# Layer norm of an attention and feed-forward kernel: the mean is subtracted from a ring of four moment buffers instead of being negated first

## What is computed

```python
x = L0_attn_x                                   # (2, 2048, 256), float32
m, v = x.mean(-1), x.var(-1)
xn = (x - m) / sqrt(v + 1e-5)                   # the layer norm, used by both branches
s = attention(xn, Wq, Wk, Wv, Wo)               # 16 heads of 16, q and k scaled to unit length,
                                                # causal window of 128 keys, linear bias
g = silu(ffn(xn, w_gate, w_up, w_down))         # 704 hidden columns; inputs and weights rounded
                                                # to a 4-bit grid in blocks of 16
out = x + s * g
```

## Time and profile before

| | |
|---|---|
| time, 3 runs | 507.41 us (507.39 to 507.47) |
| span of the profiled execution, first to last instruction | 507.1 us |
| busy: PE, DVE, ACT, POOL | 471.6 (93%), 429.2 (85%), 402.6 (79%), 415.7 (82%) us |
| PE's granted clock, mean over the span | 0.983 of full |
| shares of the chain that ended last | PE 82%, issue, DVE, ACT and POOL 1% each |
| `neg_mean` instructions | 32 of 929 on POOL |

### The profile page before, as it was taken

The page is one execution under the profiler, slowest core; times in us unless marked ns, Lnnn a source line. Parts: engine busy times, 40 slices in busy tenths (PEclk is TensorE's granted clock), DMA queues, the critical chain, the costliest instruction groups (busy, mean ns, idle before and its releaser), DMA issues.

```text
span 507.1 us, 14045 instructions
## 1 busy us (share of the span) xinstructions
PE 471.6 (93%) x4990; PEld 409.0 (81%) x4990; DVE 429.2 (85%) x865; ACT 402.6 (79%) x584; POOL 415.7 (82%) x929
## 2 busy tenths in 40 slices
PE   0367989999999999999999999999999999999997
PEld 0356768888888888888989888888898888888886
DVE  4989988889888888888989888888898888887685
ACT  1456988988888888888887888888888888888952
POOL 6554679899989989899997898989999899888651
PEclk9967999999999999999999999999999999999999
DMA  8211011222322113222222222222222221122100
GB/s 303 81 43 43 13 29 45 64 74 75 74 59 48 51 36 65 64 63 64 65 64 45 62 34 53 63 55 53 53 54 54 52 46 29 37 53 53 44 22 32
DMA packets 78276, 29.35 MB, mean 58 GB/s; under 512 B 67712, under 2 KB 77696, under 8 KB 78208
## 3 DMA queue, kind: packets, MB, share of 16 engines
q1 hardware_dynamic: 77920, 28.39, 22.2%
q10 hardware_dynamic: 288, 0.08, 0.1%
HBM read 7.49 MB, written 4.19 MB: 23 GB/s over the span
## 4 chain that ended last, share of the span: by engine, by line
PE 82%; DVE 1%; ACT 1%; issue 1%; POOL 1%; DVEq 0%; POOLq 0%
PE gt L348 12%; PE up L348 11%; PE bank_b L592 11%; PE gt L545 11%; PE bank_q L348 8%; PE bank_b L354 6%; PE gt L354 6%; PE scores L499 5%; PE gt L567 5%; PE bank_b L348 4%; PE gt L549 1%; PE up L499 1%; PE scores L348 0%; PE up L567 0%; ACT pv_t L1196 0%
## 5 line engine op out<-in xcount | busy, mean ns | idle before, releaser
L1318 ACT ACTIVATE probs<-scores 128x1024 f32<-128x1024 f32 (+1 forms) x101 | 102.5, 1015 | 3.4 <-PE scores L499 2.1
L1503 POOL TENSOR_SCALAR_AFFINE_SELECT probs<-probs 128x512 f32<-128x512 f32 x128 | 81.4, 638 | 3.0 <-ACT probs L1318 2.7
L1510 POOL TENSOR_SCALAR_AFFINE_SELECT probs<-probs 128x512 f32<-128x512 f32 x120 | 75.9, 634 | 3.7
L592 PE MATMUL bank_b<-probs,vals 128*32 128x128 f32 x1952 | 59.7, 274 | 0.4 <-DVE vals L928 0.3
L592 PEld LDWEIGHTS bank_b<-probs,vals 128*32 128x32 f32 x1952 | 51.4, 110 | 7.0 <-DVE vals L928 6.1
L1196 ACT ACTIVATE qk_stack<-bank_q 128x512 f16<-128x512 f32 x64 | 35.2, 597 | 21.8 <-DVE bank_q L907 21.8
L781 DVE TENSOR_TENSOR xT_lo<-gt,xT_hi 128x512 fp32r<-128x512 f32 (+1 forms) x34 | 22.3, 657 | 31.1 <-ACT xT_hi L1196 31.1
L545 PE MATMUL gt<-wdn_hi,hT_hi 128*128 128x256 f32 x160 | 47.8, 299 | 0.6 <-DVE hT_lo L833 0.6
L545 PE MATMUL gt<-wdn_hi,hT_lo 128*128 128x256 f32 x160 | 45.1, 282 | 0.0
L545 PE MATMUL gt<-wdn_lo,hT_hi 128*128 128x256 f32 x160 | 45.0, 281 | 0.0
L348 PE MATMUL up<-wgu_hi,xT_hi 128*128 128x352 f32 x124 | 43.2, 349 | 0.3 <-DVE h_grid L822 0.3
(11 more groups left out here) (219 smaller groups left out, 1650.9 us busy)
## 6 DMA issues: line engine op xcount, KB each, us to landing
out<-y SPq DMA_DIRECT2D x32, 128.0 KB, 2.0
x_all<-x SPq DMA_DIRECT2D x20, 128.0 KB, 2.0
x_all<-x SPq DMA_DIRECT2D x3, 512.0 KB, 4.0
x_all<-wproj SPq DMA_DIRECT2D x1, 768.0 KB, 6.7
dn_raw<-wd SPq DMA_DIRECT2D x1, 704.0 KB, 8.3
probs<-wg SPq DMA_DIRECT2D x1, 640.0 KB, 5.3
probs<-wu SPq DMA_DIRECT2D x1, 640.0 KB, 7.2
qk_slots<-qk_stack SPq DMA_TRANSPOSE x32, 3.7
```

Source lines behind the costliest of these rows:

```text
L592: done = e.matmul(pv_bank(i)[32 * n:32 * n + 32, grp * P:(grp + 1) * P], va, pr, start=part == 0, stop=part == 1 or final(i))
L1318: e.activation(probs[j % P_BUFS][:, grp, :, side(j), :], score_banks(j, grp)[:, :, :, side(j), :].rearrange("p b e h q -> p (b e) h q"), A ...
L1503: e.affine_select(out=own, in_=own, compare_op=ALU.is_ge, fill=0.0, base=0, pattern=[[0, GRP], [-1, P]], channel_multiplier=1).then_inc(s_ ...
L1510: e.affine_select(out=part, in_=part, compare_op=ALU.is_gt, fill=0.0, base=0, pattern=[[0, GRP], [1, P]], channel_multiplier=-1).then_inc( ...
```

## The change

`moments` becomes a ring of four buffers, indexed as `xn` is. `x_norm` takes the mean from there and subtracts it, so that the second instruction of `ln_parts`, the buffer `neg_mean` and the semaphore `s_neg_mean` go. `ln_moments(t)` waits only for the `x_norm` that was the last reader of its buffer, four tiles back, and for no call of POOL in the first four tiles. `x_norm(t)` waits for `s_moments` where it waited for `s_neg_mean`.

```diff
-        moments = sb("moments", [P, 2])
-        neg_mean = sb("neg_mean", [P, 2])
+        moments = sb("moments", [P, XN_BUFS, 2])
...
         def mean_col(t):
-            return neg_mean[:, 0:1] if t == 0 else neg_mean[:, 1:2]
+            return moments[:, t % XN_BUFS, 0:1]
...
             def ln_moments(t):
                 e.wait_ge(s_stats, t + 1)
-                if t >= 1:
-                    e.wait_ge(s_var, t)
-                    e.wait_ge(s_neg_mean, t)
-                e.bn_aggr(moments[:], stats[:]).then_inc(s_moments, 1)
+                if t >= XN_BUFS:
+                    e.wait_ge(s_xn, t - XN_BUFS + 1)
+                e.bn_aggr(moments[:, t % XN_BUFS, :], stats[:]).then_inc(s_moments, 1)
...
                 if t >= 2:
                     e.wait_ge(s_rs, roots(t - 3, Z_ARG))
                     e.wait_ge(s_xn, t)
-                e.tensor_scalar(ss[:, ln_col(t)], moments[:, 1:2], LN_EPS, None, ALU.add).then_inc(s_var, 1)
-                e.tensor_scalar(mean_col(t), moments[:, 0:1], -1.0, None, ALU.mult).then_inc(s_neg_mean, 1)
+                e.tensor_scalar(ss[:, ln_col(t)], moments[:, t % XN_BUFS, 1:2], LN_EPS, None, ALU.add).then_inc(s_var, 1)
...
             def x_norm(t):
                 e.wait_ge(s_rs, roots(max(t - 2, -1), ROOT))
-                e.wait_ge(s_neg_mean, t + 1)
+                e.wait_ge(s_moments, t + 1)
                 if t >= XN_BUFS:
                     e.wait_ge(s_tr_x, t - XN_BUFS + 1)
                     e.wait_ge(s_xc, chain(t - XN_BUFS, NORM))
                 e.tensor_scalar(xn[t % XN_BUFS][:], x_all[:, t % X_RING, :], mean_col(t), rsq[0][:, ln_col(t)],
-                                ALU.add, ALU.mult).then_inc(s_xn, 1)
+                                ALU.subtract, ALU.mult).then_inc(s_xn, 1)
```

More of the change, by code:

```diff
@@ L220, in build @@
             [sem(f"{n}{i}") for i in range(4)] for n in ("scores", "exp", "mask_own", "mask_prev"))
-        s_stats, s_moments, s_var, s_neg_mean, s_xn, s_rs, s_ss, s_floor, s_unit = (
-            sem(n) for n in ("s_stats", "s_moments", "s_var", "s_neg_mean", "s_xn", "s_rs", "s_ss", "s_floor", "s_unit"))
+        s_stats, s_moments, s_var, s_xn, s_rs, s_ss, s_floor, s_unit = (
+            sem(n) for n in ("s_stats", "s_moments", "s_var", "s_xn", "s_rs", "s_ss", "s_floor", "s_unit"))
         s_qk_sq, s_hi_q, s_hi_k, s_lo_qk, s_vals = (
```

## The result

The changed kernel takes 519.21 us (median of 5 runs, 518.74 to 520.12) against 507.47 us; the ratio is 1.0222, 95% interval 1.0205 to 1.0238. I had forecast 506.7. The profiled execution has a span of 518.4 us. A ratio and the quotient of two medians weigh single executions differently, and the two can be 0.1% apart.

What follows compares the result with a forecast made beforehand. PE was taken to bound the loop, with a relay of engines at the start and a POOL run ending at 72.80 us. Gains of 0.4 + 0.3 = 0.7 us gave 507.4 - 0.7 = 506.7 us, range 505.3 to 507.8.

Steps and rivals of the forecast that it cites:

- The subtraction reads the same sizes: `x_norm` on POOL: stays at 0.55 us; if 0.1 more, only tiles 0 and 4 stand on the path, costing 0.2.
- The loop: 25 `neg_mean` of 0.30 us removed from POOL between 75 and 434 us: worth 0, bounds nothing and 7.5 us.
- rival A: POOL paces the loop, so its removed work counts there: 8.2 us gained, 499.2 us; 7 in 100.
- POOL's results are just in time: Loop: POOL's root ends 0.08 us before `unit` in turn 12, yet PE does not wait for POOL.
- The start: Path to `xn(0)`: a wait of 0.22 us and a step of 0.29 go; 0.52 gained, 0.4 left by 62 us.
- `neg_mean(5)`: POOL instruction at 67.99 us, ahead of `root(3)` and `unit(3)`: its removal reaches PE whole, 0.3 us, lower bound 0.23.
- B: Start-up: return to full clock comes after `gate_mm(0)`, costing 1.6 us more, less the 0.7: 508.3 us; 10 in 100.
- C: Start-up: half-clock stretch ends before the `up` and first q/k products of 43.90 to 50.50: 504.7 us; 10 in 100.
- the low end of my sum: Lower bound of the whole gain: 0.5 us, from 0.3 at the start and 0.23 for `neg_mean(5)`.
- The new waits: `ln_moments(t)` waits for `x_norm(t - 4)`, `x_norm(t)` for `s_moments`: nothing queues behind either.

Runs made afterwards that it cites:

- experiment 1: The changed kernel with the layer norm's last step adding the mean instead of subtracting it, so it computes something else: 504.91 us, ratio 0.9954 to the kernel before.
- experiment 3: The kernel before with the negation done a second time on GpSimd, into an unread column, for tiles 7 to 31: 508.89 us, ratio 1.0018.
- experiment 2: The kernel before with the mean copied by a factor of +1 and subtracted in the layer norm's last step; buffers, waits and addresses unchanged: 527.87 us, ratio 1.0406.
- experiment 7: The changed kernel with the subtraction for tiles 7 to 31 only, and the mean added for tiles 0 to 6: 515.33 us, ratio 1.0147.
- experiment 6: The kernel before with two single additions of the root on GpSimd written as times 1 plus the constant: 506.52 us, ratio 0.998.

## Why the prediction was wrong

**The step that failed is a price: "The subtraction reads the same sizes; I take the 0.55 of `x_norm` as it is."** It measured 1.24. I had bounded it at 0.1 more, from no row. There was no subtraction with two column operands in the trace, and an honest upper bound would have compared GpSimd's other `tensor_scalar` forms. The trace had a hint: of two small instructions of the root on the same 33 columns, the one with a single addition (L1578) takes 0.32 us and the one with multiply and add (L1590) 0.23. And I priced the dearer operation on two tiles only, "the first one (of tile 0) and that of tile 4", where it was one instruction in each of 32.

**The loop, "worth: 0; bounds: nothing, and 7.5", had no slow side: this is the term through which the price came in.** I asked what less work on GpSimd would give (rival A) and did not ask what more would do. Per turn, on average over the 26 turns behind the first one:

| run | work added on GpSimd | turn longer by |
|---|---|---|
| experiment 1 | -0.31 | -0.05 |
| experiment 3 | 0.17 | 0.03 |
| changed kernel | 0.38 net (0.69 for the step, less 0.31) | 0.37 |
| experiment 2 | 0.69 | 0.65 |

So less work is worth almost nothing and more work counts almost in full. It isn't one fixed slack that is used up first, for then 0.38 would have cost at most 0.24: between 0.17 and 0.38 other instructions of GpSimd change too. Over ten turns of the changed kernel the three instructions from `ss` on take 0.22 less than before, from start to start, but one mask takes 0.19 more and `h_q` 0.12 more, so that hardly anything is left over to absorb the rest. That these stretches come from DVE's products fits the rows of experiment 3; it was not tested by moving DVE's work. "POOL's results are just in time" was in my text, and was the warning. What rival A says, that POOL paces the loop, is thus true of the changed kernel, on the slow side, where I had no rival.

**The start: right, and then lost to the other term.** I gave 0.52 us for the two removed steps, and 0.49 and 0.50 were measured from the first statistics on. That the root still meets DVE's product, as I had assumed, is so: one instruction of it takes 0.51 there as before.

**`neg_mean(5)`: right.** The moments themselves say little, since the half-clock stretches ahead of 52 us lie differently in each execution (in the profile of before the granted clock is 0.50 from 25 to 33 us and from 45 to 49, in that of the changed kernel from 45 to 51 only). The waits say it: before `unit(3)` DVE idled 0.66, and at its first `tr_tail` PE idled 0.64 (0.67 and 0.64 in experiment 3, which is alike there). With the addition it is 0.31 and 0.30 in experiment 1 and 0.34 and 0.33 in experiment 7. That is 0.3 to 0.35 less, where I had 0.31.

**The loop, with the fast step: nearly right.** The turn is mostly 14.06 to 14.11 in experiment 1 instead of 14.12 to 14.15; from the third turn to the last transposes of `tr_tail` that is 1.1 us (398.3 instead of 399.4), which I had put at nothing. And 0.3 us came from the turn at 85 to 99 us (14.12 instead of 14.41), where `unit(4)` had been waiting for the root. Another 0.2 lies outside the span: an execution's time exceeds its span by 1.9 us in the kernel before and in experiments 2 and 6, and by 1.7 to 1.8 in the changed kernel and in all the other experiments on it. Why is open. The rest of the 2.5, some 0.8, is left for the start-up, where I had 0.7; this is an estimate from the other terms.

**The clock: rivals B and C were priced on a wrong reading.** I took three times within 0.08 us of one another as a sign "that the stretches sit firmly relative to the work". They don't: executions of the kernel before alone differ by 1 us with the clock. This is the size of B, and it happens without any change. It can't be the reason for the 11.7 us, of which the loop's 9.6 are at full clock. The profiled execution of before was itself one of those at 0.983: with the 1.9 us outside its span it took about 509.0 (an estimate), so its span isn't "0.3 under the median" as I had it. Nor did the low end of my sum, 0.5, hold the 0.28 by which I had said that the start might give less. Neither changes the forecast by more than some tenths.

**The new waits** cost nothing, as forecast: with the addition neither shows among the waits.

## What to carry to other kernels

A change of the operation in an instruction is a change of its price, even at the same shape: look for a row of exactly that pair of operations on that engine, and where there is none, measure it alone or take the dearest form of the engine as the upper bound. On GpSimd that was a factor of 2.2 here. And ask in both directions how far an engine off the path is from pacing. One that never waits may be at the edge: here 0.31 us less work per turn gave 0.05, and 0.38 more cost 0.37.

## What the runs showed of the hardware that was not expected

- GpSimd's `tensor_scalar` on 128 x 256 elements with column operands: 0.55 us for add-and-multiply, multiply-and-add and multiply-and-multiply, 0.92 to 0.93 for a single operation, 1.21 to 1.24 for other pairs. Multiplying by 1 before an addition makes the addition faster (927 to 482 ns alone, with the constant as immediate; 0.31 to 0.22 at 33 columns in the kernel).
- GpSimd's `tensor_tensor` takes 0.72 for addition and subtraction alike, and DVE 0.41 for either pair of `tensor_scalar`.
- With no wait of GpSimd in its turns, small instructions beside DVE's products from SBUF took up to 0.2 us longer (`ss` 0.48 instead of 0.30, `rsq` 0.42 instead of 0.30 in the rows of experiment 3), and which ones changed with GpSimd's position by tenths of a microsecond. Of 0.17 us that were added to a turn such shifts took up 0.11.
- The same small negation on GpSimd was worth 0.31 us where it was taken out (from `ss` to the mask behind it 0.18 instead of 0.49) and cost 0.17 where a second one was put in (0.66). Why is open.
